# Windowed attention and a mixed feed-forward layer on one Trainium2 core: softmax sums turned by a transposition, and the copy of the rows of maxima one maximum later

## The chip, the cores and the metric

The kernel runs on one core of a Trainium2 chip. The time is that of the device in microseconds (us): the median of several executions, with the lowest and the highest beside it. Engines: PE (TensorE) multiplies and transposes, and loads its weights (PEld) while it does; DVE (VectorE) works elementwise and reduces; ACT (ScalarE) evaluates functions and can issue DMAs; POOL (GpSimd) works elementwise; SP (SyncE) issues DMAs.

## The reference, cut to what matters

```
x : 4 x 2048 x 512
h = layernorm(x);  q, k, v = split(h @ w_qkv)                # 16 heads of 32, 16 windows of 128 tokens
scores[q, key] = (q * 32**-0.5) . k                          # keys: the window before, its own, the one after
attn = softmax(scores, over the keys);  o = attn @ v
x = x + layernorm(o)
x = x + layernorm(ffn(layernorm(x)))                         # weights mixed of 8 experts by a gate, one mix per batch
```

The change lies in the softmax and its normalisation: for each query the maximum of its scores is taken off before the exponential, and the output is divided by the sum of the exponentials.

## The kernel before, in words

The program has three stages. Up to about 570 us it makes q, k and v; each operand is kept as a high and a low part and every product as three. From there to about 1305 us it does attention. The rest is the gate and the feed-forward layer, which the diff doesn't touch.

**The attention loop.** The work is cut into 16 rounds (4 batches by 4 groups of 4 heads), each round into 8 steps of two windows: 128 steps, each with 2 x 4 = 8 units (window, head). The order is written out by hand, engine by engine. The loop `for T in range(STEPS + LAG)` stands once for each engine, and in its pass T several steps are under way:

- **Step T+3: scores and maxima.** PE multiplies queries by keys (`score`, L628) into three PSUM banks used in turn; DVE takes each unit's negated maximum (`reduce`, L493). Score s waits for maximum s-3, whose bank it takes. A unit has 384 keys, or 256 in the first and the last window of a batch.
- **Step T+2: maxima turned.** PE transposes the 128 x 8 maxima into `ps_turn` (`turn_max`, L655) and DVE copies the 8 rows to SBUF (`copy_rows`, L501, then `rows_done`). `send_row` (L196) puts them by DMA under the queries, in partition 96 of `q_st`, the row of window 0 of the step from ACT and that of window 1 from SP. Both wait for `rows_done` first. On ACT it stands behind the fifth exponential (x = 4) of the pass, and x = 5, 6 and 7 stand behind it.
- **Step T: keys by queries, exponentials.** PE multiplies again with the operands exchanged and with the row of maxima as a 97th row, so that the maximum comes off in the product (`keys`, L647), into three other banks; ACT takes exp (`weights`, L421). Product x waits for exponential x-3, also across steps: products 0, 1 and 2 of the next step wait for exponentials 5, 6 and 7 of this one. Product 0 of a step waits for SP's row, product 4 for ACT's row of the step after.
- **Step T-2: values, sums, output.** PE multiplies values by exponentials (`values`, L676) and, from the totals that POOL adds up, makes the sums (`sums`, L684): row 32h+i of `ps_out[:, 2]` has the sums of head h and window i, other rows are zero. ACT copies all to `out_t` (`copy_out`, L428). `turn_out` transposes the two windows (L694) and turns the sums with a product by `pick`, a 128 x 8 selection matrix (L695); it waits for `rows_done` of step T+2, since both use `ps_turn`. DVE inverts the 8 columns of sums (`normalise`, L505) and multiplies (L509); SP stores.

PE's order in a pass: score 0, product 0, score 1, products 1 and 2, score 2, values and sums, `turn_max`, score 3, product 3, score 4, products 4 and 5, scores 5 and 6, product 6, `turn_out`, product 7, score 7. DVE's: maxima 0, 1, 2, the copy of rows, maxima 3 to 7, `normalise`. ACT's: exponentials 0, 1, 2, `copy_out`, exponentials 3 and 4, the DMA of a row, exponentials 5, 6, 7.

Of the kernel before, what the change touches and what calls it, by code (L numbers as in the profile page):

```python
# [5 lines left out]
ALU = mybir.AluOpType  # L6
ACT = mybir.ActivationFunctionType
AX_X = mybir.AxisListType.X
F32 = mybir.dt.float32
F32R = mybir.dt.float32r  # L10

P = 128
D = 512
HEADS = 16
E = D // HEADS
# [7 lines left out]
QH = 4  # L23
# [20 lines left out]
def attention_programs(nc, ident, eps, power, unused, x, w_qkv, qk_dram, v_dram, o_dram):  # L44
# [15 lines left out]
    UNITS = 2 * QH  # L60
    FRONT = AHEAD * UNITS // GROUPS
    PIECES = (0, P, D, 2 * D, 3 * D)
    with ExitStack() as ctx:
        def sb(name, shape, dt, stack=ctx):
            return stack.enter_context(nc.sbuf_tensor("a_" + name, shape, dt))
# [5 lines left out]
            return nc.alloc_semaphore("a_" + name)  # L71

        neg_max = sb("neg_max", [P, 2, 2, QH], F32)
        pick = sb("pick", [P, 2 * QH], F32)
        inv_sum = sb("inv_sum", [P, 2, 2 * QH], F32)
        ones = sb("ones", [P, 2, E], F32)
        max_rows = sb("max_rows", [2 * QH, 2, WIN], F32R)
        q_st = sb("q_st", [P, QH, SEQ], F32R)
# [2 lines left out]
        ps_turn = psum("ps_turn", [P, 4, WIN])  # L81
# [23 lines left out]
        out_t = sb("out_t", [P, 2, 3, WIN], F32)  # L105
        out = sb("out", [P, 2, 2, QH * E], F32)
# [37 lines left out]
        const_done = sem("const_done")  # L144
# [13 lines left out]
        inv_done = sem("inv_done")  # L158
        norm_done = sem("norm_done")
        out_turned = sem("out_turned")  # L160
# [130 lines left out]
        def gpsimd(pool, along):  # L291
            pool.memset(ident[:, :], 0.0).then_inc(front_const, 1)
            pool.memset(eps[:, :], EPS).then_inc(front_const, 1)
            pool.memset(power[:, :], -0.5).then_inc(front_const, 1)
            pool.wait_ge(front_const, 3)
            pool.affine_select(out=ident[:, :], in_=ident[:, :], compare_op=ALU.not_equal, fill=1.0,
                               base=0, pattern=[[-1, P]], channel_multiplier=1).then_inc(front_const, 1)

            for s in range(SLOTS):
                pool.sem_inc(qk_stored[s], 16)  # L300
            for p in range(2):
                pool.sem_inc(v_stored[p], 16 * QUADS)
            pool.memset(ones[:, :, :], 0.0).then_inc(const_done, 1)
            pool.wait_ge(const_done, 1)
            for i in range(2):
                pool.memset(ones[:, i, i:i + 1], 1.0).then_inc(const_done, 1)
                pool.wait_ge(const_done, 2 + i)
            pool.memset(pick[:, :], 0.0).then_inc(const_done, 1)
            pool.wait_ge(const_done, 4)
            pool.affine_select(out=pick[:, :], in_=pick[:, :], compare_op=ALU.not_equal, fill=1.0,  # L310
                               base=0, pattern=[[-1, 2], [-E, QH]], channel_multiplier=1).then_inc(const_done, 1)
            pool.wait_ge(const_done, 5)
            pool.wait_ge(xn_done, 1)
            pool.memset(k_st[STACK:STACK + 1, :, :].bitcast(F32), 1.0).then_inc(const_done, 1)

            def parts(m):
                w = m % W
                lo, hi = span(w)
                return [probs[:, (m - w + kb) % PROBS, :, (w - span(kb)[0]) * WIN:(w - span(kb)[0] + 1) * WIN]
                        for kb in range(lo, hi)]  # L320

            def first_two(g, i):
                m = 2 * g + i
                lo, hi = span(m % W)
                p = parts(m)
                pool.wait_ge(exp_done, QH * (m - m % W + lo + 2))
                if g >= 2:
                    pool.wait_ge(pv_done, g - 1)
                add = pool.tensor_tensor(total[:, g % 2, i], p[0], p[1], ALU.add)  # L329
                add.then_inc(part_summed if len(p) > 2 else summed, 1)  # L330

            def third(g, i):
                m = 2 * g + i
                lo, hi = span(m % W)
                p = parts(m)
                if len(p) > 2:
                    pool.wait_ge(exp_done, QH * (m - m % W + hi))
                    pool.wait_ge(part_summed, threes(m))
                    pool.tensor_tensor(total[:, g % 2, i], total[:, g % 2, i], p[2], ALU.add).then_inc(summed, 1)  # L339

            for g in range(STEPS):
                along(g)
                first_two(g, 0)
                if g % HALF == HALF - 1:
                    third(g, 0)
                    first_two(g, 1)
                else:
                    first_two(g, 1)
                    third(g, 0)
                    third(g, 1)  # L350
# [93 lines left out]
        def vector(dve, along):  # L444
# [57 lines left out]

            def normalise(g):
                dve.wait_ge(out_turned, g + 1)
                dve.reciprocal(inv_sum[:, g % 2, :], ps_turn[:, 3, 0:2 * QH]).then_inc(inv_done, 1)  # L505
                dve.wait_ge(inv_done, g + 1)
                if g >= 2:
                    dve.wait_ge(out_stored[g % 2], 16 * (g // 2))
                dve.tensor_tensor(out[:, g % 2].rearrange("p w (h e) -> p (w h) e", h=QH),  # L509
                                  ps_turn[:, 1:3, :].rearrange("p w (h e) -> p (w h) e", h=QH),  # L510
                                  inv_sum[:, g % 2, :].unsqueeze(2).to_broadcast([P, 2 * QH, E]),
                                  ALU.mult).then_inc(norm_done, 1)

            dve.wait_ge(x_half_loaded, 16)
# [34 lines left out]
                    copy_rows(1)  # L549
            for T in range(STEPS + LAG):  # L550
                if there(T + AHEAD):
                    for s in range(3):
                        reduce(T + AHEAD, s)
                if there(T + AHEAD - 1):
                    copy_rows(T + AHEAD - 1)
                if there(T + AHEAD):
                    for s in range(3, UNITS):
                        reduce(T + AHEAD, s)
                if there(T - LAG):
                    normalise(T - LAG)  # L560
                along(T)

        def tensor(pe, along):
# [124 lines left out]
            def turn_out(g):  # L688
                pe.wait_ge(out_copied, g + 1)
                pe.wait_ge(rows_done, min(g + LAG + AHEAD, STEPS))  # L690
                if g >= 1:
                    pe.wait_ge(norm_done, g)
                for i in range(2):
                    pe.transpose(ps_turn[:, 1 + i, :], out_t[:, g % 2, i, :], ident[:, :])  # L694
                pe.matmul(ps_turn[:, 3, 0:2 * QH], out_t[:, g % 2, 2, :], pick[:, :],  # L695
                          start=True, stop=True, skip_group_check=True).then_inc(out_turned, 1)

            def scores(T, units):
                if there(T + AHEAD):
# [9 lines left out]
            for k in range(KD):  # L709
                for t in range(TILES):  # L710
                    mm = pe.transpose(opening[k][:, t * P:(t + 1) * P], xn[:, t, k * P:(k + 1) * P], ident[:, :])
                mm.then_inc(turned, 1)
            pe.wait_ge(w_lo_done, 1)
            for k in range(KD):
# [3 lines left out]
                mm = pe.matmul(acc[0][:, :], w_lo[:, k, 0:P], xt_hi[:, 0, k, :], start=False, stop=(k == KD - 1))  # L718
# [9 lines left out]
                chunk(i, 0)  # L728
                chunk(i, 1)
            chunk(PAIRS - 1, 0)  # L730
            pe.wait_ge(const_done, 6)
            for g in range(GROUPS):
                group(CHUNKS - 1, 1, g)
                for y in range(FRONT * g, FRONT * (g + 1)):
# [1282 lines left out]
```

## Time and profile before

| | |
|---|---|
| time, median of 3 runs | 2935.83 us (2935.25 to 2944.34) |
| the profiled execution: its own time | 2944.44 us |
| the profiled execution: its span, first to last instruction | 2942.7 us |
| PE busy | 2878.3 us, 98% |
| PE weight loads busy | 2399.2 us, 82% |
| DVE busy | 1994.3 us, 68% |
| ACT busy | 1733.9 us, 59% |
| POOL busy | 856.6 us, 29% |
| chain that ended last, by engine | PE 86%, DMA 6%, DVE 4%, ACT 2% |

How to read it: a busy time is the union of an engine's instructions. A matmul's record starts when it is taken up, which can be before its weights are in, and its end is modelled; so PE can be waiting for a moment inside a busy stretch, and the loads (PEld) show that better. A "q" behind an engine's name (ACTq) is its sequencer, which issues DMAs. "Idle before" is the engine's idle time in front of an instruction and what ended it.

### The profile page before, as it was taken

To read this page: it belongs to the slowest core of one execution; us is meant where nothing else is said; L and a number is where in the kernel's file an instruction comes from. 1 tells how busy PE (TensorE), PEld (TensorE's weight loads), DVE (VectorE), ACT (ScalarE), POOL (GpSimd) and SP (SyncE) were. 2 spreads that over 40 slices of the span, in tenths; PEclk is the share of its full clock that TensorE was granted. 3 is DMA by queue.
4 is the path that set the end of the run, shared out by engine and by line. 5 is a ranking of instruction groups with operands and counts; after the bars stand their busy time and mean duration, and the time that the engine had idled before them with its cause. 6 is when DMAs were issued, how large, how long until landed. Compare 5 with 4: busy or idle time off the path is not lost.

```text
span 2942.7 us, 55697 instructions
## 1 busy us (share of the span) xinstructions
PE 2878.3 (98%) x20380; PEld 2399.2 (82%) x20380; DVE 1994.3 (68%) x3769; ACT 1733.9 (59%) x3385; POOL 856.6 (29%) x715
## 2 busy tenths in 40 slices
PE   8999999999999999989989999999999999999998
PEld 6888888788888888777867888888888888888886
DVE  5333333488888887778868766886769766786664
ACT  3222222367776766666546666766667666686666
POOL 1000000188888887874400000400005000040003
PEclk9999999999999999999999999999999999999999
DMA  6554555688788879959998866986769765895642
GB/s 215 185 171 171 186 188 193 215 193 197 191 199 197 196 193 219 220 167 393 400 389 327 295 208 221 348 324 204 245 212 404 272 204 201 287 390 201 233 136 86
DMA packets 361430, 697.11 MB, mean 237 GB/s; under 512 B 26576, under 2 KB 127056, under 8 KB 361184
## 3 DMA queue, kind: packets, MB, share of 16 engines
q1 hardware_dynamic: 335456, 629.63, 66.8%
q10 hardware_dynamic: 17424, 32.24, 3.1%
q0 software_dynamic: 8304, 31.98, 2.7%
q8 instruction: 151, 2.47, 0.4%
q14 instruction: 95, 0.78, 0.1%
HBM read 525.45 MB, written 167.78 MB: 236 GB/s over the span
## 4 chain that ended last, share of the span: by engine, by line
PE 86%; DMA 6%; DVE 4%; ACT 2%; issue 1%; POOL 1%; ACTq 0%; SPq 0%; DVEq 0%; POOLq 0%
PE a_acc L577 17%; PE e_hid L1397 8%; PE e_hid L1399 8%; PE e_hid L1398 8%; PE e_acc L1414 8%; PE e_acc L1416 8%; PE e_acc L1415 8%; PE a_ps_score L628 6%; PE a_ps_keys L647 6%; PE a_ps_out L676 5%; DMA a_q_st<-a_max_rows 2%; DMA a_gate_att<-o_scratch 2%; PE a_ps_out L684 2%; DVE a_gate_stats L1665 1%; PE a_turn L572 1%
## 5 line engine op out<-in xcount | busy, mean ns | idle before, releaser
L1787 DVE SCALAR_TENSOR_TENSOR e_part<-e_ring,e_g_cols,e_part 128x512 f32<-128x512 f32 x896 | 644.8, 775 | 5.2 <-DMA e_ring<-mix_rows 2.8
L493 DVE TENSOR_REDUCE a_neg_max<-a_ps_score 128x1 f32<-128x384 f32 (+1 forms) x1024 | 491.6, 527 | 63.0 <-PE a_ps_score L628 51.9
L329 POOL TENSOR_TENSOR a_total<-a_probs 128x512 f32<-128x512 f32 x256 | 323.9, 1282 | 592.4 <-ACT a_probs L421 592.2
L421 ACT ACTIVATE a_probs<-a_ps_keys 128x384 f32<-128x384 f32 (+1 forms) x1024 | 429.6, 477 | 53.9 <-PE a_ps_keys L647 24.2
L1811 DVE TENSOR_TENSOR e_u_lo<-e_u,e_u_hi 128x512 fp32r<-128x512 f32 x256 | 180.6, 706 | 372.0 <-ACT e_u_hi L1545 371.9
L1541 ACT ACTIVATE e_u<-e_hid,e_mb 128x512 f32<-128x512 f32 x256 | 176.9, 691 | 427.7 <-PE e_hid L1399 418.2
L1270 POOL TENSOR_SCALAR e_var<-e_moments 128x4 f32<-128x4 f32 x15 | 6.7, 447 | 1269.6 <-DVE e_moments L1823 1269.0
L628 PE MATMUL a_ps_score<-a_k_st,a_q_st 96*128 96x384 f32 (+1 forms) x1024 | 333.9, 361 | 3.5 <-DMA a_q_st<-qk_scratch 2.5
L647 PE MATMUL a_ps_keys<-a_q_st,a_k_st 97*128 97x384 f32 (+1 forms) x1024 | 314.8, 350 | 12.2 <-DMA a_q_st<-a_max_rows 11.1
L339 POOL TENSOR_TENSOR a_total<-a_total,a_probs 128x512 f32<-128x512 f32 x224 | 286.3, 1280 | 67.0 <-ACT a_probs L421 64.3
L473 DVE TENSOR_TENSOR a_qk<-a_acc,a_qk 128x512 fp32r<-128x512 f32 x128 | 88.1, 690 | 308.1 <-ACT a_qk L370 308.1
L1558 ACT ACTIVATE e_sums<-e_acc 128x512 f32<-128x512 f32 x508 | 289.2, 595 | 8.3 <-PE e_acc L1416 5.1
L1569 ACT ACTIVATE e_acc<-e_sums 128x512 f32<-128x512 f32 x448 | 263.7, 614 | 0.0
L370 ACT ACTIVATE a_qk<-a_acc 128x512 fp32r<-128x512 f32 x128 | 76.2, 598 | 259.0 <-PE a_acc L577 255.6
L628 PEld LDWEIGHTS a_ps_score<-a_k_st,a_q_st 96*128 96x128 f32 x1024 | 193.0, 191 | 36.3 <-DVE a_neg_max L493 22.7
L647 PEld LDWEIGHTS a_ps_keys<-a_q_st,a_k_st 97*128 97x128 f32 x1024 | 192.4, 192 | 24.1 <-DMA a_q_st<-a_max_rows 15.4
L577 PE MATMUL a_acc<-a_xt_hi,a_w_hi 128*128 128x512 f32 x508 | 202.5, 399 | 1.1 <-DVE a_qk L473 0.6
L1397 PE MATMUL e_hid<-e_y_hi,e_wb_hi 128*128 128x512 f32 x512 | 200.1, 391 | 2.5 <-DVE e_wb_lo L1806 2.5
L1414 PE MATMUL e_acc<-e_wb_hi,e_u_hi 128*128 128x512 f32 x512 | 199.9, 390 | 1.2 <-ACT e_acc L1569 1.1
L1397 PE MATMUL e_hid<-e_y_hi,e_wa_hi 128*128 128x512 f32 x512 | 200.2, 391 | 0.0
L1414 PE MATMUL e_acc<-e_wa_hi,e_u_hi 128*128 128x512 f32 x512 | 199.4, 389 | 0.7 <-issue 0.6
L1399 PE MATMUL e_hid<-e_y_hi,e_wa_lo 128*128 128x512 f32 x512 | 199.9, 390 | 0.0
(158 smaller groups left out, 6508.5 us busy)
## 6 DMA issues: line engine op xcount, KB each, us to landing
e_ring<-mix_rows SPq DMA_DIRECT2D x558, 512.0 KB, 5.5
qk_scratch<-a_qk SPq DMA_DIRECT2D x128, 512.0 KB, 3.2
a_k_st<-qk_scratch SPq DMA_DIRECT2D x180, 256.0 KB, 4.4
a_q_st<-qk_scratch SPq DMA_DIRECT2D x180, 256.0 KB, 4.4
v_scratch<-a_v SPq DMA_DIRECT2D x64, 256.0 KB, 3.0
a_v_sb<-v_scratch SPq DMA_DIRECT2D x64, 256.0 KB, 4.9
o_scratch<-a_out SPq DMA_DIRECT2D x128, 128.0 KB, 2.9
x_scratch<-a_gate_x POOLq DMA_DIRECT2D x16, 1024.0 KB, 10.0
```

Of the source, the lines that this page charges most:

```text
L329: add = pool.tensor_tensor(total[:, g % 2, i], p[0], p[1], ALU.add)
L339: pool.tensor_tensor(total[:, g % 2, i], total[:, g % 2, i], p[2], ALU.add).then_inc(summed, 1)
L421: act.activation(probs[:, m % PROBS, h, 0:(hi - lo) * WIN], ps_keys[x % TRIO][:, 0:(hi - lo) * WIN], ACT.Exp, scale=SCALE).then_inc(exp_do ...
L493: dve.tensor_reduce(neg_max[:, g % 2, i, h:h + 1], ps_score[y % TRIO][:, 0:(hi - lo) * WIN], AX_X, ALU.max, negate=True).then_inc(reduced, 1)
L577: mm = pe.matmul(out, lhs, rhs, start=(n == 0), stop=(n == len(terms) - 1))
L628: pe.matmul(ps_score[y % TRIO][:, 0:(hi - lo) * WIN], q_st[0:STACK, h, w * WIN:(w + 1) * WIN], k_st[0:STACK, h, lo * WIN:hi * WIN], start= ...
L647: pe.matmul(ps_keys[x % TRIO][:, 0:(hi - lo) * WIN], k_st[0:STACK + 1, h, w * WIN:(w + 1) * WIN], q_st[0:STACK + 1, h, lo * WIN:hi * WIN], ...
L1397: pe.matmul(hid[s % 4][:, :], w_hi(n)[:, 0, cols], y_hi[:, slot, k, :], start=(k == 0), stop=False)
L1399: mm = pe.matmul(hid[s % 4][:, :], w_lo(n)[:, 0, cols], y_hi[:, slot, k, :], start=False, stop=(k == KD - 1))
L1414: pe.matmul(acc[t][:, :], u_hi[:, s % 3, cols], w_hi(n)[:, 1, :], start=False, stop=False, skip_group_check=True)
L1558: act.activation(sums[:, runs[r][1], t, :], acc[t][:, :], ACT.Copy).then_inc(copied, 1)
L1787: dve.scalar_tensor_tensor(out=part[:, n % 2, half, :], in0=ring[:, slot, :], scalar=g_cols[:, b, e:e + 1], in1=so_far, op0=ALU.mult, op1= ...
```

## The change

The third column block of `turn_out` becomes a transposition like the other two; `pick`, its building on POOL and its share of the counts of `const_done` go; the reciprocal reads the sums where the transposition leaves them (column 32h+i) and writes them in order of windows. DVE's copy of the rows moves from behind maximum 2 to behind maximum 3.

```diff
--- before.py
+++ after.py
@@ -71,8 +71,7 @@
             return nc.alloc_semaphore("a_" + name)
 
         neg_max = sb("neg_max", [P, 2, 2, QH], F32)
-        pick = sb("pick", [P, 2 * QH], F32)
-        inv_sum = sb("inv_sum", [P, 2, 2 * QH], F32)
+        inv_sum = sb("inv_sum", [P, 2, 2, QH], F32)
         ones = sb("ones", [P, 2, E], F32)
         max_rows = sb("max_rows", [2 * QH, 2, WIN], F32R)
         q_st = sb("q_st", [P, QH, SEQ], F32R)
@@ -305,11 +304,6 @@
             for i in range(2):
                 pool.memset(ones[:, i, i:i + 1], 1.0).then_inc(const_done, 1)
                 pool.wait_ge(const_done, 2 + i)
-            pool.memset(pick[:, :], 0.0).then_inc(const_done, 1)
-            pool.wait_ge(const_done, 4)
-            pool.affine_select(out=pick[:, :], in_=pick[:, :], compare_op=ALU.not_equal, fill=1.0,
-                               base=0, pattern=[[-1, 2], [-E, QH]], channel_multiplier=1).then_inc(const_done, 1)
-            pool.wait_ge(const_done, 5)
             pool.wait_ge(xn_done, 1)
             pool.memset(k_st[STACK:STACK + 1, :, :].bitcast(F32), 1.0).then_inc(const_done, 1)
 
@@ -502,13 +496,13 @@
 
             def normalise(g):
                 dve.wait_ge(out_turned, g + 1)
-                dve.reciprocal(inv_sum[:, g % 2, :], ps_turn[:, 3, 0:2 * QH]).then_inc(inv_done, 1)
+                dve.reciprocal(inv_sum[:, g % 2], ps_turn[:, 3, :].rearrange("p (h e) -> p e h", e=E)[:, 0:2, :]).then_inc(inv_done, 1)
                 dve.wait_ge(inv_done, g + 1)
                 if g >= 2:
                     dve.wait_ge(out_stored[g % 2], 16 * (g // 2))
                 dve.tensor_tensor(out[:, g % 2].rearrange("p w (h e) -> p (w h) e", h=QH),
                                   ps_turn[:, 1:3, :].rearrange("p w (h e) -> p (w h) e", h=QH),
-                                  inv_sum[:, g % 2, :].unsqueeze(2).to_broadcast([P, 2 * QH, E]),
+                                  inv_sum[:, g % 2].rearrange("p w h -> p (w h)").unsqueeze(2).to_broadcast([P, 2 * QH, E]),
                                   ALU.mult).then_inc(norm_done, 1)
 
             dve.wait_ge(x_half_loaded, 16)
@@ -549,12 +543,12 @@
                     copy_rows(1)
             for T in range(STEPS + LAG):
                 if there(T + AHEAD):
-                    for s in range(3):
+                    for s in range(4):
                         reduce(T + AHEAD, s)
                 if there(T + AHEAD - 1):
                     copy_rows(T + AHEAD - 1)
                 if there(T + AHEAD):
-                    for s in range(3, UNITS):
+                    for s in range(4, UNITS):
                         reduce(T + AHEAD, s)
                 if there(T - LAG):
                     normalise(T - LAG)
@@ -690,10 +684,9 @@
                 pe.wait_ge(rows_done, min(g + LAG + AHEAD, STEPS))
                 if g >= 1:
                     pe.wait_ge(norm_done, g)
-                for i in range(2):
-                    pe.transpose(ps_turn[:, 1 + i, :], out_t[:, g % 2, i, :], ident[:, :])
-                pe.matmul(ps_turn[:, 3, 0:2 * QH], out_t[:, g % 2, 2, :], pick[:, :],
-                          start=True, stop=True, skip_group_check=True).then_inc(out_turned, 1)
+                for i in range(3):
+                    mm = pe.transpose(ps_turn[:, 1 + i, :], out_t[:, g % 2, i, :], ident[:, :])
+                mm.then_inc(out_turned, 1)
 
             def scores(T, units):
                 if there(T + AHEAD):
@@ -728,7 +721,7 @@
                 chunk(i, 0)
                 chunk(i, 1)
             chunk(PAIRS - 1, 0)
-            pe.wait_ge(const_done, 6)
+            pe.wait_ge(const_done, 4)
             for g in range(GROUPS):
                 group(CHUNKS - 1, 1, g)
                 for y in range(FRONT * g, FRONT * (g + 1)):
```

## Rows read from the trace of the kernel before

Times in a timeline are us from the span's start. Pass 62 of the attention loop is the one whose `turn_max` starts at 910.79 us, pass 63 starts so at 916.33, 61 at 905.39 and 60 at 900.04.

**Rows 1.** The page's head line.
```profile
span 2942.7 us, 55697 instructions
```

**Rows 2.** Busy time by engine, 640 to 1150 us (columns named in the first line).
```profile
core 0: us, PE busy (x) PEld busy (x) DVE busy (x) ACT busy (x) POOL busy (x), PEclk, DMA share, GB/s
640.00:1150.00 510.00, 506.85 (x7732) 439.57 (x7731) 419.81 (x1027) 358.03 (x842) 437.21 (x350) 1.00 0.82 197
```

**Rows 3.** Timeline, PE and its weight loads: start, duration (us), work, count, [idle before].
```profile
910.79 0.08 PEld L655 LDWEIGHTS a_ps_turn<-ident,a_neg_max 128*8 128x8 f32 x1 [0.20 <-issue]
...
910.83 0.42 PE L628 MATMUL a_ps_score<-a_k_st,a_q_st 96*128 96x384 f32 x1
...
912.00 0.19 PEld L628 LDWEIGHTS a_ps_score<-a_k_st,a_q_st 96*128 96x128 f32 x1 [0.20 <-DVE a_neg_max L493]
...
912.28 0.34 PE L647 MATMUL a_ps_keys<-a_q_st,a_k_st 97*128 97x384 f32 x1
...
912.46 0.38 PE L694 MATMUL a_ps_turn<-ident,a_out_t 128*128 128x128 f32 x2
...
912.68 0.17 PE L695 MATMUL a_ps_turn<-a_pick,a_out_t 128*128 128x8 f32 x1
...
913.08 0.34 PE L628 MATMUL a_ps_score<-a_k_st,a_q_st 96*128 96x384 f32 x1
...
913.82 0.19 PEld L647 LDWEIGHTS a_ps_keys<-a_q_st,a_k_st 97*128 97x128 f32 x1
...
914.07 0.19 PEld L628 LDWEIGHTS a_ps_score<-a_k_st,a_q_st 96*128 96x128 f32 x1
...
914.44 0.11 PEld L676 LDWEIGHTS a_ps_out<-a_probs,a_v_sb 128*32 128x32 f32 x2 [0.19 <-issue]
...
916.33 0.08 PEld L655 LDWEIGHTS a_ps_turn<-ident,a_neg_max 128*8 128x8 f32 x1 [0.20 <-issue]
```

**Rows 4.** Timeline, DVE, the same step.
```profile
911.21 0.28 DVE L501 CAST a_max_rows<-a_ps_turn 8x128 fp32r<-8x128 f32 x1 [0.75 <-PE a_ps_turn L655]
...
911.41 0.53 DVE L493 TENSOR_REDUCE a_neg_max<-a_ps_score 128x1 f32<-128x384 f32 x1
...
911.88 0.54 DVE L493 TENSOR_REDUCE a_neg_max<-a_ps_score 128x1 f32<-128x384 f32 x1
...
913.46 0.56 DVE L493 TENSOR_REDUCE a_neg_max<-a_ps_score 128x1 f32<-128x384 f32 x1
```

**Rows 5.** Timeline, ACT, the same step.
```profile
911.82 0.58 ACTq L196 DMA_DIRECT2D a_q_st<-a_max_rows  x1
...
912.45 0.49 ACT L421 ACTIVATE a_probs<-a_ps_keys 128x384 f32<-128x384 f32 x1
...
912.83 0.48 ACT L421 ACTIVATE a_probs<-a_ps_keys 128x384 f32<-128x384 f32 x1
...
913.28 0.49 ACT L421 ACTIVATE a_probs<-a_ps_keys 128x384 f32<-128x384 f32 x1
```

**Rows 6.** Timeline, DVE and SP, the step before it.
```profile
905.80 0.28 DVE L501 CAST a_max_rows<-a_ps_turn 8x128 fp32r<-8x128 f32 x1 [1.22 <-PE a_ps_turn L655]
...
906.01 0.40 DVE L493 TENSOR_REDUCE a_neg_max<-a_ps_score 128x1 f32<-128x256 f32 x1
...
906.11 0.58 SPq L196 DMA_DIRECT2D a_q_st<-a_max_rows  x1
```

**Rows 7.** Timeline, other kinds of step, DVE, ACT and PE weight loads.
```profile
900.45 0.28 DVE L501 CAST a_max_rows<-a_ps_turn 8x128 fp32r<-8x128 f32 x1 [0.75 <-PE a_ps_turn L655]
...
903.51 0.13 PEld L676 LDWEIGHTS a_ps_out<-a_probs,a_v_sb 128*32 128x32 f32 x4 [0.20 <-issue]
...
908.91 0.12 PEld L676 LDWEIGHTS a_ps_out<-a_probs,a_v_sb 128*32 128x32 f32 x3 [0.18 <-ACT a_probs L421]
...
917.93 0.66 ACT L421 ACTIVATE a_probs<-a_ps_keys 128x256 f32<-128x256 f32 x2 [0.17 <-issue]
...
919.85 0.12 PEld L676 LDWEIGHTS a_ps_out<-a_probs,a_v_sb 128*32 128x32 f32 x3 [0.18 <-ACT a_probs L421]
```

**Rows 8.** Waits, 600 to 1270 us: total, times, longest (us).
```profile
PEld a_ps_keys L647 <- DMA a_q_st<-a_max_rows: 13.9, 13, 3.1
```

## The prediction

> **What bounds the kernel now.** I read the busy times of a stretch of the attention loop first, then the timeline of one pass engine by engine, then the waits. The stretch shows PE busy 506.85 of 510 us at a granted clock of 1.00, DVE 419.81, ACT 358.03, POOL 437.21 [rows 2]. PE looks like the only bound, and a change that shortens PE's work should pay in full. But PE's record covers stalls: what is to be seen is in the loads. In pass 62 (5.54 us, from 910.79 to 916.33) the load of score 6 starts at 912.00 after 0.20 idle, released by DVE [rows 3]: maximum 3 ran from 911.41 to 911.95 [rows 4]. The load of the next product 2 starts at 913.82 [rows 3], 0.05 after exponential 7 ended at 913.77 (913.28 + 0.49) [rows 5]. The load of the next score 2 starts at 914.07 [rows 3], 0.05 after maximum 7 ended at 914.02 [rows 4]. So PE is handed from one engine to another three times a pass, with almost nothing to spare: a gain on PE alone goes only as far as the next of these.
>
> **Turn-out on PE.** Two transpositions take 0.38 us and one 0.27 (its length when alone, mostly latency), so they follow each other at 0.11. The two passes of the pick product begin at 912.68; product 7 behind them really begins 0.175 before score 7, whose matmul starts at 913.08 (0.175 is the pace of a 384-key matmul: product 6 at 912.28, first transposition at 912.46). That is 912.91, so the pick product costs 0.23 [rows 3]. A third transposition costs 0.11 at the pace of the two, with its own 128 x 128 load like theirs. Saved on PE: 0.12 a pass. The cost is bounded from both sides by 0.11 (that pace) and 0.23 (no gain, if it took two passes as the product does); I take 0.11, the row of the same operation.
>
> **Reciprocal, multiplication, constants.** The reciprocal still makes 8 values per partition, now read 32 apart; between nothing and a few hundredths, on DVE where 0.75 us are idle before each copy [rows 4]. POOL's two instructions for `pick` run before the first layernorm is done, and PE asks for the constants only at the last chunk: nothing.
>
> **Copy behind maximum 3, on DVE.** Now the copy starts at 911.21 and maximum 3 at 911.41, 0.20 behind; maxima follow at 0.46 (911.41, 911.88) and take 0.54 [rows 4]. After the change maximum 3 starts as soon as score 3 is there: its matmul ends at 910.83 + 0.42 = 911.25 [rows 3], and DVE needs 0.04 more (score 7 ends at 913.42, maximum 7 starts at 913.46) [rows 3, 4]. So maximum 3 runs 911.29 to 911.82, 0.13 earlier; score 6 no longer stalls for it (a gain of about 0.13 on PE). The copy starts 0.46 behind, 911.75, and ends at 912.03, where it ended at 911.49: 0.54 later. Maximum 4 starts 0.20 behind it, 911.95 (before 911.88), maximum 7 at 913.35 if score 7 is there, and PE, 0.25 ahead by then, has it there. It ends at 913.90 (before 914.02): by DVE, score 2 could go 0.11 earlier.
>
> **Who waits for the copy.** Three: SP's DMA, PE's turn-out, ACT's DMA. *SP*: its row goes out 0.54 later and is wanted almost a pass and a half later; `store` behind it in SP's queue waits for `normalise` anyway. *PE*: turn-out may start from about 912.09; score 6 and product 6 bring PE there at about 912.15. Hidden, with 0.06 to spare. *ACT*: its DMA starts at 911.82, as soon as exponential 4 has been handed over, takes 0.58, and exponential 5 starts at 912.45, 0.05 behind its end; exponentials 5 and 6 are 0.38 apart [rows 5]. So ACT already loses 0.2 a pass to the issue, and everything behind the DMA waits with it. By a row of the step before, a DMA that waited for the copy starts 0.03 after it (copy 905.80 + 0.28, SP's DMA 906.11) [rows 6]. After the change ACT's DMA can't start before 912.03 + 0.03 = 912.06, 0.24 later than now. It ends at 912.64, exponential 5 starts at 912.69, 6 at 913.07, 7 at 913.46 (product 7 is long there), ending at 913.95. The load of the next product 2 then starts at 914.00 instead of 913.82. That is the new stall.
>
> No row of before has ACT waiting in front of its DMA, so what such a wait holds up is not shown. The Trainium skill (DMA: Bandwidth & Descriptors, Anatomy of one DMA) says the wait of a DMA is done on the issuing sequencer, which agrees with my reading. The same section puts the dispatch at about 50 ns; the row has 0.58 us, and the row decides. With 50 ns exponential 5 would not be delayed at all, and the sum would be that of the first rival.
>
> **The sum for an ordinary pass.** A stalled load lets its matmul begin 0.11 after it starts (load of score 6 at 912.00, product 6 at 912.28 less 0.175) [rows 3]. Now: score 2 at 914.07 + 0.11 = 914.18. After: product 2 at 914.11, score 2 0.175 later, 914.285. Values, sums and the next `turn_max` follow in fixed distance (914.44, 916.33). Change: **+0.10 us**, against the 0.25 that PE gained and the 0.11 that DVE allowed. Passes 0, 1, 2, 3 and 6 of a round are of this kind: +0.52.
>
> **The other passes of a round.** In pass 4 maxima of 256 keys let PE run on: values start 3.47 after `turn_max` (903.51, and 900.45 - 0.41 = 900.04) [rows 7], in pass 62 3.65. ACT's chain is as long as in pass 62, and puts them at 3.65 + 0.10 less 0.05 for the shorter score 2: +0.22. In pass 5 maximum 3 takes 0.40 [rows 6] and its score is 0.06 shorter, so the copy ends earlier (1.04 after `turn_max`, not 1.24) and ACT's delay is 0.1: values at 3.55 against 3.52 (905.39, 908.91) [rows 7]: +0.03. In pass 7 the exponentials behind the DMA have 256 keys and follow at 0.28 [rows 7]; ACT would be done in time, DVE ends maximum 7 as late as now; values at 3.52 (919.85) [rows 7] stay: 0. A round: 0.52 + 0.22 + 0.03 = 0.77 us, 16 rounds: **+12.3 us**.
>
> **Rows landing late.** Product 4 waited 13 times for a row to land, 13.9 us in all [rows 8]. ACT's row leaves 0.24 later while the pass grows by 0.10, so each such wait deepens by 0.14, 1.8 us; nothing at the low end, 6 us at the high end if rows that just make it now fall behind (twice as many waits, each 0.24). I take +1.8.
>
> Sum: +14 us. The profiled execution took 2944.44 us for a span of 2942.7 [rows 1], and goes to 2958.5; it is 8.6 above the median of the runs shown, 2935.83, which goes to **2950**. About 0.3% (9 us) is what a measurement of this kernel can tell from no change.
>
> **Rivals.**
> *ACT's DMA holds nobody up* (faster). If ACT had its slack elsewhere, or exponentials 5 to 7 could go on, DVE would be next: score 2 0.11 earlier in five passes, about 0.1 in passes 4 and 5, none in 7: 0.75 a round, -12 us, 2924. For it: PE's and DVE's rows both allow it. Against: exponential 5 starts 0.05 behind the DMA's end in every pass. It decides once the delay on ACT is under the slack of product 2 and score 2, about 0.13; it needs the copy to end before 911.92, and even with no latency at all (911.25 + 0.46 + 0.28 = 911.99) it doesn't. Chance 0.13.
> *The two cancel* (no change). The ACT chain is shorter than I have it by up to 0.1, as when exponentials close up to 0.35 behind one another; 2931 to 2943. Chance 0.19.
> *The copy is held till maximum 3 is finished* (slower still). Rows show the next DVE instruction 0.07 before the end of the last [rows 4], but always of maxima. Then ACT is 0.07 later in seven passes of eight, +8 us, and PE's turn-out loses its 0.06 of cover as well: 2958. Chance 0.15. The Trainium skill (VectorE: DVE Perf Modes, The DRAIN you can't avoid) has the next instruction wait for the pipe to empty, which would be this case; the overlap of the maxima speaks against it.
> *The third transposition is no cheaper than the pick product*: no effect on the sum, since PE waits for ACT by then; it is inside the forecast.
>
> **The numbers.** The forecast has 0.53, the case still slower 0.15, no change 0.19, faster 0.13. Slower by over 0.3%: 0.53 + 0.15 less what falls below 2944.6, and some of the cancelling case above it: 0.68. Range 2932 to 2962: from most of the cancelling case to late rows on top of the held copy; it leaves the faster rival out.
>
> **What would show it.** In the changed kernel's ordinary pass: maximum 3 starts 0.49 after `turn_max` and the copy at 0.95; ACT's DMA at 1.26 instead of 1.03; exponential 5 at 1.89 instead of 1.66; no idle before the load of score 6; a new wait of product loads on exponentials; turn-out in three steps of 0.11; pass length 5.63 instead of 5.54, and 5.58 instead of 5.36 in pass 4. It would be wrong if exponential 7 ended less than 3.04 after `turn_max`, or if the DMA of ACT took less than 0.58.

## The result, and the profile after

| | before | after |
|---|---|---|
| time, median (lowest to highest) | 2944.03 us (2935.25 to 2951.69, 8 runs) | 2953.94 us (2946.92 to 2958.25, 8 runs) |
| ratio to before | | **1.0029**, 95% interval 1.0015 to 1.0043 |
| profiled execution: own time, span | 2944.44, 2942.7 us | 2950.66, 2948.8 us |

The change makes the kernel slower, by 8.5 us (0.0029 x 2944), between 4.4 and 12.7. The median of before over eight runs is 8 us above that of the three runs known ahead of the prediction; the ratio counts.

The page after, against [rows 1]: the head line, the busy times, and the two groups in which something new stands.

```profile
span 2948.8 us, 55438 instructions
...
PE 2882.6 (98%) x20252; PEld 2375.6 (81%) x20252; DVE 1986.2 (67%) x3769; ACT 1719.0 (58%) x3385; POOL 854.6 (29%) x713
...
L487 DVE TENSOR_REDUCE a_neg_max<-a_ps_score 128x1 f32<-128x384 f32 (+1 forms) x1024 | 495.0, 528 | 168.4 <-PE a_ps_score L622 166.7
...
L641 PEld LDWEIGHTS a_ps_keys<-a_q_st,a_k_st 97*128 97x128 f32 x1024 | 190.1, 190 | 55.2 <-ACT a_probs L415 23.4
```

The maxima (L487) now have 166.7 us of idle time before them that scores ended; in front of the copy there was such idle time before [rows 4]. The loads of products (L641) wait for exponentials (L415), a wait that was hardly there before. The busy times in the stretch of [rows 2]:

```profile
core 0: us, PE busy (x) PEld busy (x) DVE busy (x) ACT busy (x) POOL busy (x), PEclk, DMA share, GB/s
640.00:1150.00 510.00, 507.39 (x7588) 419.15 (x7584) 406.53 (x1014) 340.47 (x829) 433.64 (x347) 1.00 0.81 193
```

PE looks just as busy as before (507.39 against 506.85 us): this view doesn't show the loss. ACT and DVE get fewer instructions done in the same 510 us (829 against 842, and 1014 against 1027). Pass 62, PE and its loads, against [rows 3]:

```profile
917.93 0.08 PEld L649 LDWEIGHTS a_ps_turn<-ident,a_neg_max 128*8 128x8 f32 x1 [0.20 <-issue]
...
919.03 0.19 PEld L622 LDWEIGHTS a_ps_score<-a_k_st,a_q_st 96*128 96x128 f32 x1
...
919.48 0.49 PE L688 MATMUL a_ps_turn<-ident,a_out_t 128*128 128x128 f32 x3
...
920.20 0.19 PEld L622 LDWEIGHTS a_ps_score<-a_k_st,a_q_st 96*128 96x128 f32 x1 [0.20 <-issue]
...
921.12 0.19 PEld L641 LDWEIGHTS a_ps_keys<-a_q_st,a_k_st 97*128 97x128 f32 x1 [0.20 <-ACT a_probs L415]
...
923.55 0.08 PEld L649 LDWEIGHTS a_ps_turn<-ident,a_neg_max 128*8 128x8 f32 x1 [0.20 <-issue]
```

The pass takes 5.62 us from `turn_max` to `turn_max` (before 5.54). The load of score 6 comes 1.10 after `turn_max` (before 1.21), and three transpositions take 0.49, that is 0.11 more than two. Then the gain goes: the load of the next score 0 comes 0.20 after the engine fell idle ("issue": the view names no releaser; maximum 5, which it needs, had just ended at 920.09), and the load of product 2, at 3.19, waits 0.20 for an exponential; before it came at 3.03. DVE, against [rows 4]:

```profile
918.42 0.56 DVE L487 TENSOR_REDUCE a_neg_max<-a_ps_score 128x1 f32<-128x384 f32 x1 [1.06 <-PE a_ps_score L622]
...
918.89 0.27 DVE L495 CAST a_max_rows<-a_ps_turn 8x128 fp32r<-8x128 f32 x1
...
920.48 0.54 DVE L487 TENSOR_REDUCE a_neg_max<-a_ps_score 128x1 f32<-128x384 f32 x1
```

Maximum 3 starts at 0.49, the copy at 0.96, its end is at 1.23; maximum 7 starts at 2.55. ACT, against [rows 5]:

```profile
919.19 0.58 ACTq L195 DMA_DIRECT2D a_q_st<-a_max_rows  x1
...
919.82 0.49 ACT L415 ACTIVATE a_probs<-a_ps_keys 128x384 f32<-128x384 f32 x1 [0.35 <-PE a_ps_keys L641]
...
920.58 0.50 ACT L415 ACTIVATE a_probs<-a_ps_keys 128x384 f32<-128x384 f32 x1
```

The DMA starts at 1.26 (before 1.03), 0.03 behind the copy's end. ACT then sits idle 0.35 us while its sequencer issues, exponential 5 starts at 1.89 and exponential 7 at 2.65, ending at 3.15. The view names "PE a_ps_keys" for the idle time of exponential 5, but product 5 had ended long before; it is the DMA in front of it. The waits from 600 to 1270 us, the second row against [rows 8]:

```profile
PEld a_ps_keys L641 <- ACT a_probs L415: 20.2, 103, 0.2
...
PEld a_ps_keys L641 <- DMA a_q_st<-a_max_rows: 17.3, 17, 1.9
...
PEld a_ps_score L622 <- DVE a_neg_max L487: 2.8, 15, 0.2
```

The same view of before:

```profile
PEld a_ps_score L628 <- DVE a_neg_max L493: 19.9, 91, 0.4
...
PEld a_ps_keys L647 <- ACT a_probs L421: 0.2, 1, 0.2
```

Products now wait 103 times for an exponential, 20.2 us, where it was once; scores wait for maxima 15 times, 2.8 us, where it was 91 times and 19.9 us.

### The profile page after: what moved, and what is told of

It reads as the page before. It is cut to its first block, busy times and chain, and to the rows that moved or that the text cites. A ratio compares the mean times of both kernels' runs of the same rounds, so it can differ in the third digit from the quotient of the medians.

```text
span 2948.8 us, 55438 instructions
## 1 busy us (share of the span) xinstructions
PE 2882.6 (98%) x20252; PEld 2375.6 (81%) x20252; DVE 1986.2 (67%) x3769; ACT 1719.0 (58%) x3385; POOL 854.6 (29%) x713
## 4 chain that ended last, share of the span: by engine, by line
PE 84%; DMA 6%; DVE 5%; issue 2%; ACT 2%; POOL 1%; ACTq 0%; SPq 0%; DVEq 0%; POOLq 0%
PE a_acc L571 17%; PE e_acc L1407 7%; PE e_hid L1390 7%; PE e_hid L1392 7%; PE e_hid L1391 7%; PE e_acc L1408 7%; PE e_acc L1409 7%; PE a_ps_keys L641 6%; PE a_ps_score L622 6%; PE a_ps_out L670 5%; DMA a_q_st<-a_max_rows 3%; DMA a_gate_att<-o_scratch 2%; PE a_ps_out L678 2%; PE a_ps_turn L688 1%; DVE e_part L1780 1%
## 5 line engine op out<-in xcount | busy, mean ns | idle before, releaser
L487 DVE TENSOR_REDUCE a_neg_max<-a_ps_score 128x1 f32<-128x384 f32 (+1 forms) x1024 | 495.0, 528 | 168.4 <-PE a_ps_score L622 166.7
L415 ACT ACTIVATE a_probs<-a_ps_keys 128x384 f32<-128x384 f32 (+1 forms) x1024 | 413.6, 479 | 65.7 <-PE a_ps_keys L641 58.1
L641 PE MATMUL a_ps_keys<-a_q_st,a_k_st 97*128 97x384 f32 (+1 forms) x1024 | 336.3, 364 | 15.8 <-DMA a_q_st<-a_max_rows 12.2
L641 PEld LDWEIGHTS a_ps_keys<-a_q_st,a_k_st 97*128 97x128 f32 x1024 | 190.1, 190 | 55.2 <-ACT a_probs L415 23.4
L1391 PE MATMUL e_hid<-e_y_lo,e_wa_hi 128*128 128x512 f32 x512 | 199.8, 390 | 0.0
```

The costliest lines, as they stand in the source:

```text
L415: act.activation(probs[:, m % PROBS, h, 0:(hi - lo) * WIN], ps_keys[x % TRIO][:, 0:(hi - lo) * WIN], ACT.Exp, scale=SCALE).then_inc(exp_do ...
L487: dve.tensor_reduce(neg_max[:, g % 2, i, h:h + 1], ps_score[y % TRIO][:, 0:(hi - lo) * WIN], AX_X, ALU.max, negate=True).then_inc(reduced, 1)
L641: pe.matmul(ps_keys[x % TRIO][:, 0:(hi - lo) * WIN], k_st[0:STACK + 1, h, w * WIN:(w + 1) * WIN], q_st[0:STACK + 1, h, lo * WIN:hi * WIN], ...
L1391: pe.matmul(hid[s % 4][:, :], w_hi(n)[:, 0, cols], y_lo[:, slot, k, :], start=False, stop=False)
```

## The experiments

Each ratio is against the kernel before, run on the same chip. "A round" is the sum over the 8 kinds of pass of the median distance between `turn_max` starts in that kernel's profile; times 16 it gives the price of the passes alone. (In e3 the median of pass 2, 5.67 us, is raised by passes that wait; up to `turn_max` 104 it is 5.49.) The columns on the right split one profiled execution at `turn_max` 10, 104 and 127, with the granted clock of the last stretch. `turn_max` n turns the maxima of step n and lies in pass n-2; it is at pass 102, behind `turn_max` 104, that SP begins to load for the gate beside the attention loop.

| kernel | turn | copy behind | ACT's row | a round, us | x16, against before | measured ratio (interval) | 10 to 104, us | 104 to 127, us | clock, 104 to 127 |
|---|---|---|---|---|---|---|---|---|---|
| before | pick | 2 | behind x=4 | 43.40 | | | 512.2 | 146.5 | 0.93 |
| after | transposed | 3 | x=4 | 44.16 | +12.1 | 1.0029 (1.0015, 1.0043) | 520.4 | 138.8 | 1.00 |
| e1 | transposed | 2 | x=4 | 42.63 | -12.3 | 0.9970 (0.9959, 0.9980) | 504.3 | 141.1 | 0.98 |
| e8 (as e1) | transposed | 2 | x=4 | 42.62 | -12.5 | 0.9978 (0.9968, 0.9989) | 506.1 | 149.0 | 0.92 |
| e2 | pick | 3 | x=4 | 44.18 | +12.4 | 1.0027 (1.0017, 1.0038) | 519.5 | 139.0 | 0.99 |
| e3 | transposed | 3 | from SP | 42.91 | -7.8 | 0.9985 (0.9976, 0.9993) | 507.2 | 144.5 | 0.94 |
| e4 | transposed | 3 | x=5 | 42.77 | -10.1 | 0.9982 (0.9973, 0.9990) | 504.6 | 144.3 | 0.95 |
| e5 | transposed | 4 | x=4 | 47.63 | +67.6 | 1.0201 (1.0184, 1.0218) | 560.6 | 146.9 | 0.97 |
| e6 | pick | 3 | from SP | 42.97 | -7.0 | 1.0007 (0.9995, 1.0018) | 509.9 | 138.7 | 0.99 |
| e7 | transposed | 2 | x=3 | 43.17 | -3.8 | 0.9992 (0.9983, 1.0001) | 508.3 | 143.7 | 0.94 |
| e9 | transposed | 2 | x=5 | 42.52 | -14.2 | 0.9973 (0.9964, 0.9981) | 501.9 | 151.1 | 0.92 |
| e10 | transposed | 2 | from SP | 42.54 | -13.8 | 0.9984 (0.9974, 0.9993) | 504.7 | 144.7 | 0.94 |

### The two parts alone (e1, e8, e2)

e1 and e8, the same kernel measured on two chips, are the changed kernel with the copy back at its place:

```diff
-                    for s in range(4):
+                    for s in range(3):
                         reduce(T + AHEAD, s)
                 if there(T + AHEAD - 1):
                     copy_rows(T + AHEAD - 1)
                 if there(T + AHEAD):
-                    for s in range(4, UNITS):
+                    for s in range(3, UNITS):
                         reduce(T + AHEAD, s)
```

> The sums turned by the third transposition, the copy of the rows left behind maximum 2. Theory (ACT's row DMA, which waits for the copy, is what costs in the full change): the DMA starts at 1.03 after turn_max as before, so the 0.115 us saved on PE in the turn-out goes through: score 7 and with it maximum 7 come 0.115 earlier, ACT's chain still has room (exponential 7 ends at 2.92, it may end at 2.95). Ordinary pass 5.42 us instead of 5.53, kernel 10 to 14 us faster than before, ratio 0.995 to 0.997. Rival (a gain on PE is worth nothing in this loop, because DVE and ACT hand work to it): pass 5.53, ratio 1.000. Second rival (the third transposition is what makes the full change slower): ratio over 1.002.

> The third transposition alone once more, as the measure for the two runs beside it: ratio 0.996 to 0.998, ordinary pass 5.42 us. Both theories say the same of it.

Pass 62 of e1, `turn_max`, the load of the next score 2 and the next `turn_max`:

```profile
904.74 0.08 PEld L649 LDWEIGHTS a_ps_turn<-ident,a_neg_max 128*8 128x8 f32 x1 [0.20 <-issue]
...
907.91 0.19 PEld L622 LDWEIGHTS a_ps_score<-a_k_st,a_q_st 96*128 96x128 f32 x1
...
910.17 0.08 PEld L649 LDWEIGHTS a_ps_turn<-ident,a_neg_max 128*8 128x8 f32 x1 [0.20 <-issue]
```

5.43 us, and score 2 at 3.17 (before 3.27), 0.05 behind maximum 7. The transposition alone saves 0.11 us an ordinary pass, all that it saves on PE, and the ratios are 0.9970 and 0.9978. The rivals fall: PE's gain counts, and the transposition isn't what costs.

e2 is the kernel before with the same edit the other way round.

> The copy behind maximum 3, the sums turned by the pick product as before. Theory: ACT's chain sets the pass, which does not see the turn-out: DMA of the row at 1.26, exponential 5 at 1.89, pass 5.63 us, the same as in the full change; kernel 12 us slower than before (ratio 1.004), within 2 us of the full change. Rival (the two parts add, each with its own price on PE): the full change less the gain of the transposition, pass 5.75, 20 to 26 us slower, ratio 1.007 to 1.009.

A round is 44.18 us against 44.16 of the full change, the ratio 1.0027 against 1.0029. With the copy behind maximum 3, and ACT's DMA where it is, the transposition is worth nothing: the parts don't add, ACT sets the pass and the turn-out lies beside it. (1.004 was expected; the passes alone would give it.)

### ACT's wait taken away, two ways (e3, e4)

e3:

```diff
                 if there(T + AHEAD - 1):
-                    send_row(sp, T + AHEAD - 1, 1)
+                    for i in range(2):
+                        send_row(sp, T + AHEAD - 1, i)
...
-                    if x == 4 and there(T + AHEAD - 1):
-                        send_row(act, T + AHEAD - 1, 0)
```

> The full change, with both rows of a step sent by SP and none by ACT. Theory: ACT no longer waits nor issues, exponential 5 starts at 1.44, and product 2 no longer waits for exponential 7. Next is DVE: maximum 6 ends at 2.62 and sets score 1, three matmuls later score 2; ordinary pass 5.47 us, kernel 6 us faster than before (ratio 0.998) and 18 us faster than the full change. Rival (the loss comes from the copy being late for PE's turn-out or from the rows landing late): pass 5.63 or waits of products on DMAs of more than 30 us in all, ratio 1.003 or more, since copy and rows are as late as in the full change or later.

Pass 62 of e3: `turn_max`, exponentials 4 and 5, the load of score 1, the next `turn_max`:

```profile
907.88 0.08 PEld L648 LDWEIGHTS a_ps_turn<-ident,a_neg_max 128*8 128x8 f32 x1 [0.20 <-issue]
...
908.94 0.87 ACT L416 ACTIVATE a_probs<-a_ps_keys 128x384 f32<-128x384 f32 x2
...
910.56 0.19 PEld L621 LDWEIGHTS a_ps_score<-a_k_st,a_q_st 96*128 96x128 f32 x1
...
913.34 0.08 PEld L648 LDWEIGHTS a_ps_turn<-ident,a_neg_max 128*8 128x8 f32 x1 [0.20 <-issue]
```

Exponential 5 follows 4 at once. The load of score 1 comes at 2.68, released by maximum 6 as the theory had it, and the pass takes 5.46. The copy is as late as in the full change and the row that ACT sent leaves no earlier, and the loss is gone.

e4 only moves the DMA behind the next exponential:

```diff
-                    if x == 4 and there(T + AHEAD - 1):
+                    if x == 5 and there(T + AHEAD - 1):
```

> The full change, with ACT's DMA of the row one exponential later, behind x = 5. The issue still costs ACT its 0.58 us, but the wait for the copy (till 1.23) is over by then. Theory: exponential 5 at 1.44, DMA at 1.41 to 1.99, exponential 6 at 2.04, 7 at 2.43, its end at 2.92 sets nothing; ordinary pass 5.47 us like with the rows sent by SP, 6 us faster than before from the passes, given back in part by rows that leave 0.38 later than before (0 to 6 us): ratio 0.998 to 1.000. Rival (it is the cost of issuing on ACT, not the wait in front of it): as the full change, ratio 1.003, pass 5.63.

```profile
905.24 0.08 PEld L649 LDWEIGHTS a_ps_turn<-ident,a_neg_max 128*8 128x8 f32 x1 [0.20 <-issue]
...
906.51 0.58 ACTq L195 DMA_DIRECT2D a_q_st<-a_max_rows  x1
...
906.67 0.50 ACT L415 ACTIVATE a_probs<-a_ps_keys 128x384 f32<-128x384 f32 x1
...
910.71 0.08 PEld L649 LDWEIGHTS a_ps_turn<-ident,a_neg_max 128*8 128x8 f32 x1 [0.20 <-issue]
```

ACT's DMA still starts at 1.27 and takes 0.58, but exponential 5 starts at 1.43, and the pass takes 5.47. What costs is that the wait for the copy, and behind it the 0.58 us of the issue, stand in front of exponential 5; the same issue one place later costs nothing that the pass shows. The late copy by itself costs little: with ACT's DMA at x=4 it makes a round 1.53 us longer (44.16 against 42.63), at x=5 only 0.25 (42.77 against 42.52, e9 below).

### The copy later still (e5)

```diff
-                    for s in range(4):
+                    for s in range(5):
...
-                    for s in range(4, UNITS):
+                    for s in range(5, UNITS):
```

> The full change with the copy of the rows one maximum later still, behind maximum 4. Theory (ACT's DMA waits for the copy): the copy ends at 1.70 after turn_max instead of 1.23, the DMA runs from 1.73 to 2.31, exponential 5 starts at 2.36, 7 ends at 3.61, the load of product 2 starts at 3.66 instead of 3.20: ordinary pass 6.10 us (5.635 in the full change, 5.53 before), a round longer by 3.6 us than in the full change, 58 us in all, so 70 us slower than before from the passes alone, ratio 1.020 to 1.024, the lower end since passes that wait for a landing row anyway have less to lose. Rival (PE's turn-out, which waits for the same copy, sets the pass): it would start 0.32 us later, ordinary pass 5.95, ratio 1.016 or less. Second rival (what costs is one instruction more in front of DVE's copy, not when it ends): 5.74, ratio 1.008.

Pass 62: `turn_max`, the copy, ACT's DMA, the load of the next product 2, the next `turn_max`:

```profile
944.90 0.08 PEld L649 LDWEIGHTS a_ps_turn<-ident,a_neg_max 128*8 128x8 f32 x1 [0.20 <-issue]
...
946.33 0.27 DVE L495 CAST a_max_rows<-a_ps_turn 8x128 fp32r<-8x128 f32 x1
...
946.63 0.58 ACTq L195 DMA_DIRECT2D a_q_st<-a_max_rows  x1
...
948.57 0.19 PEld L641 LDWEIGHTS a_ps_keys<-a_q_st,a_k_st 97*128 97x128 f32 x1 [0.20 <-ACT a_probs L415]
...
951.00 0.08 PEld L649 LDWEIGHTS a_ps_turn<-ident,a_neg_max 128*8 128x8 f32 x1 [0.20 <-issue]
```

The copy starts at 1.43, the DMA at 1.73, product 2 waits for exponential 7 till 3.67, the pass takes 6.10 us. Every time that the theory gave for this pass is there. PE's turn-out does wait for the copy here (its first load starts at 1.77, in after at 1.38), but it would set 5.95; both rivals fall. A round is 3.47 us longer than in the full change (3.6 expected).

### Is the transposition worth something without ACT's wait? (e6)

e6 is e2 with the rows sent by SP, as in e3.

> The copy behind maximum 3 and the sums turned by the pick product, both rows sent by SP. Theory: without ACT's wait DVE sets the pass through maximum 6 and score 1, which lie behind PE's turn-out with time to spare, so the transposition is worth nothing here: pass 5.47 us and ratio 0.998 to 0.999, as with the third transposition. Rival (PE's own time sets the pass once ACT is out of the way): 0.115 us longer, 5.58, ratio 1.002 to 1.003.

Two `turn_max` of an undisturbed pass of the same kind:

```profile
864.82 0.08 PEld L654 LDWEIGHTS a_ps_turn<-ident,a_neg_max 128*8 128x8 f32 x1 [0.20 <-issue]
...
870.29 0.08 PEld L654 LDWEIGHTS a_ps_turn<-ident,a_neg_max 128*8 128x8 f32 x1 [0.20 <-issue]
```

5.47 us, as forecast: in an ordinary pass the transposition is worth nothing here. But the ratio is 1.0007 where 0.998 to 0.999 was expected, and e3 has 0.9985. Passes 4 and 5 are 0.12 and 0.07 us longer than in e3, which explains 3 us of the 6 (16 x 0.19). What makes the rest was not separated.

### The rows' landing (e7, e9, e10)

e7 is e1 with `x == 3` for ACT's DMA.

> The third transposition, the copy behind maximum 2, and ACT's DMA of the row one exponential earlier, behind x = 3, where the copy has just ended: DMA at 0.71 instead of 1.03, exponential 4 at 1.33, 5 at 1.71, 7 ends at 2.97. Theory of the row that lands late (product 4 waits for ACT's row, some 17 us in all when passes are short): rows leave 0.3 us earlier, which takes 5 to 7 us off these waits, against 0.03 us a pass on ACT's chain, 3 us: ratio to before 0.995 to 0.997, at or below that of the transposition alone (0.997), waits of products on rows under 12 us. Rival (these waits are set by the DMA queues' load and not by when the row leaves): waits stay at 17 us or more and the ratio is 0.998.

```profile
908.95 0.08 PEld L649 LDWEIGHTS a_ps_turn<-ident,a_neg_max 128*8 128x8 f32 x1 [0.20 <-issue]
...
909.67 0.58 ACTq L195 DMA_DIRECT2D a_q_st<-a_max_rows  x1
...
910.68 0.48 ACT L415 ACTIVATE a_probs<-a_ps_keys 128x384 f32<-128x384 f32 x1
...
914.41 0.08 PEld L649 LDWEIGHTS a_ps_turn<-ident,a_neg_max 128*8 128x8 f32 x1 [0.20 <-issue]
```

```profile
PEld a_ps_keys L641 <- DMA a_q_st<-a_max_rows: 11.2, 10, 2.7
```

The waits of products on rows fall to 11.2 us as expected, but exponential 5 starts at 1.73 and the pass takes 5.46, not 5.45, and passes 4 and 5 of a round got 0.12 and 0.15 longer, which the expectation had left out: a round costs 0.54 us more than in e1, 8.5 us in all instead of 3. The ratio, 0.9992, where 0.995 to 0.997 was expected (0.998 by the rival), agrees with the price of the passes, 0.9987.

e9 is e1 with `x == 5`; e10 is e1 with the rows from SP.

> The third transposition, the copy behind maximum 2, and ACT's DMA of the row behind x = 5. On ACT the same work stands in front of exponential 7 (it starts at 2.42 in either order), so the ordinary pass stays at 5.42 us; only the row leaves 0.37 us later. Theory of the late rows (what a kernel gains or loses beside its passes is in passes that wait for a row): waits of products on rows rise by 5 to 7 us over the run beside it, ratio 0.002 above it. Rival (the row has time enough, these waits come and go with the chip): ratio as in the run beside it, within 0.001.

The waits of products on rows, first in e9, then in e8 beside it:

```profile
PEld a_ps_keys L641 <- DMA a_q_st<-a_max_rows: 14.6, 18, 2.8
```

```profile
PEld a_ps_keys L641 <- DMA a_q_st<-a_max_rows: 20.3, 16, 2.9
```

The row leaves at 1.20 after `turn_max` instead of 1.03: 0.17 later, not 0.37, since ACT hands exponential 5 over sooner there. So the test was weaker than planned. The waits are shorter in this profile, not longer, and 0.9973 is within 0.001 of 0.9978: no sign that a later departure costs, but half the dose. With e7 on the other side, whether the time of departure sets these waits stays open.

> The third transposition, the copy behind maximum 2, both rows sent by SP. ACT has nothing to issue: exponential 7 no longer sets product 2, and what is left is DVE (maximum 7 ends at 3.11, score 2 at 3.17): ordinary pass 5.42 us as with the transposition alone, passes 4 and 5 of a round shorter by 0.1 or so, 3 us in all. SP sends the row that ACT sent at 0.71 in even passes and about 0.9 in odd ones, behind its loads, so rather earlier than ACT. Theory: ratio 0.994 to 0.996, 3 to 6 us faster than the run beside it. Rival (ACT's issue was hidden, only its wait for the copy cost anything): ratio as in the run beside it, within 0.001.

A round is 0.08 us shorter than in e8 (1.3 us in all, 3 expected), and 0.9984 is not below 0.9978. ACT's issue without the wait was hidden, as the rival said. What three kernels with both rows from SP give back beside their passes, 3.4 us (e3) to 9.1 (e6 and e10), isn't explained. In these three product 4 waits for its row most often, 23 times in e3, 27 in e6 and 24 in e10, against 9 to 20 in the others; no run tests whether that is the reason.

### Where the passes' price went

In each of the eleven comparisons the measured ratio lies on the side of less effect than the price of the passes, by 1 to 9 us (e6 even changes its sign). The split at pass 102 shows where to look. First before, then after, from `turn_max` 10 to 104 and from 104 to 127:

```profile
core 0: us, PE busy (x) PEld busy (x) DVE busy (x) ACT busy (x) POOL busy (x), PEclk, DMA share, GB/s
617.33:1129.54 512.21, 510.48 (x7802) 442.97 (x7799) 422.68 (x1034) 361.28 (x846) 440.71 (x353) 1.00 0.81 195
1129.54:1276.05 146.51, 135.17 (x1908) 115.45 (x1905) 112.46 (x271) 93.92 (x215) 121.39 (x101) 0.93 0.90 216
```

```profile
619.55:1139.94 520.39, 517.78 (x7708) 427.32 (x7705) 415.13 (x1034) 348.18 (x846) 441.11 (x353) 1.00 0.81 193
1139.94:1278.71 138.77, 127.25 (x1885) 104.10 (x1881) 110.07 (x271) 91.66 (x215) 120.65 (x100) 1.00 0.93 226
```

In the first 94 passes the change costs 520.4 - 512.2 = 8.2 us, close to 94/8 x 0.76 = 8.9. The last 23 take 146.5 before and 138.8 after. That is mostly the clock: the granted clock of TensorE was 0.93 in the last stretch of before and 1.00 in that of after. In before it is at 0.50, the lower of its two levels, for some 20 us, beside the three longest waits of PE for a DMA (2.83, 3.09 and 1.97 us). The second of these, and four of the microseconds behind it:

```profile
1183.54 0.29 PEld L647 LDWEIGHTS a_ps_keys<-a_q_st,a_k_st 97*128 97x128 f32 x1 [3.09 <-DMA a_q_st<-a_max_rows]
```

```profile
1186.00:1190.00 4.00, 4.00 (x33) 3.48 (x37) 2.93 (x6) 1.89 (x5) 2.51 (x2) 0.50 0.82 164
```

This pass is 6.9 us longer than the median of its kind, for a wait of 3.1. In after no wait is longer than 1.9 us and the clock stays at 1.00. The column of clocks in the table puts the other kernels in the same order: the last 23 passes take 138.7 to 141.1 us at 0.98 to 1.00, 143.7 to 146.5 at 0.93 to 0.95, 149.0 and 151.1 at 0.92 (e5, whose passes are 0.5 us longer, 146.9 at 0.97). Times the clock, as an estimate of what they would have taken without its loss, they come to about 136.3 before and 138.8 after: 2.5 apart, where 23/8 x 0.76 = 2.2 is the price of the passes. For e5 it is 142.5, 6 us above before where its passes ask for 12, and for e1 138.3, above before where its passes ask for less. So a difference between two profiles in this stretch says little of the change, and the passes' price is paid in it only in part. The clock doesn't explain why the medians fall short: the mean clock of a kernel's executions differs from that of before beside it by at most 0.0007 (0.9934 against 0.9927 for e1, 0.9929 against 0.9936 for e8), which is 2 us, in either direction.

There the DMA engines are busier (0.90 and 0.93 against 0.81) with the loads for the gate beside the rest, and products wait for rows. What such a wait does, in one pass of after: the copy, the load of product 4, ACT's DMA.

```profile
1170.59 0.27 DVE L495 CAST a_max_rows<-a_ps_turn 8x128 fp32r<-8x128 f32 x1
...
1171.88 0.19 PEld L641 LDWEIGHTS a_ps_keys<-a_q_st,a_k_st 97*128 97x128 f32 x1 [1.77 <-DMA a_q_st<-a_max_rows]
...
1172.37 0.58 ACTq L195 DMA_DIRECT2D a_q_st<-a_max_rows  x1
```

The copy ends at 1170.86, but product 4 waits for its row till 1171.88, exponential 4 for product 4, and ACT's DMA goes out at 1172.37, 1.5 us after the copy. In such a pass it doesn't matter when the copy is made. The lengths agree: six passes of before with such a wait are each longer than the median of its kind by about 0.19 us less than the wait (1.46 waited, 1.27 longer, behind `turn_max` 106), and ten of after by about 0.30 less (1.36 and 1.06). So with the same wait the pass is as long in both, and the 0.10 of the change isn't paid. That is under 2 us in all 17 waits of after, and no run shows how much of the rest it makes.

## Why the prediction was right or wrong

- **Direction, mechanism, size.** Slower was forecast with 0.68, by ACT's DMA waiting for the copy. The pass: maximum 3 forecast at 0.49 and found at 0.49, copy 0.95 and 0.96, DMA 1.26 and 1.26, exponential 5 1.89 and 1.89, product 2's load 3.20 and 3.19, pass 5.63 and 5.62. Between them e2, e3, e4 and e5 tell this mechanism from PE's turn-out, from late rows and from the issue by itself. The rival in which ACT's DMA holds nobody up fell with exponential 5 at 1.89. It was also priced too high: in e3 and e4, where ACT holds nobody up, a round is 0.49 and 0.63 us shorter than before, not 0.75, since maximum 6 then holds score 1, a wait that the prediction left out.
- **Turn-out.** 0.12 saved by the transposition: three take 0.49, against 0.38 for two and 0.23 for the pick product, 0.61; e1 shows it in the time.
- **Copy held?** The rival of a copy held 0.07 till maximum 3 is finished fell: maximum 3 runs 918.42 to 918.98, the copy starts at 918.89. The overlap is as between maxima, so this copy was not made to wait for the pipe to empty. The section of the Trainium skill that the prediction names for that rule (VectorE: DVE Perf Modes, The DRAIN you can't avoid) adds that a next instruction that is not held starts earlier; the prediction left this out, and the trace agrees with it: the copy starts 0.08 us before the end of the maximum.
- **The other passes.** Forecast +0.22, +0.03 and 0 for 4, 5 and 7; medians +0.22, +0.04 and -0.03. A round: 0.77 forecast, 0.76 measured.
- **Rows landing late: the term that was off.** "I take +1.8" assumed that a pass that waits for a row pays the longer pass and a wait 0.14 deeper. The waits did grow, from 13.9 us in 13 times to 17.3 in 17, but not deeper (1.07 and 1.02 us each), and over the kernels run they are 8.0 to 22.0, so one profile can't confirm the size. The longer pass isn't paid there: ACT's DMA stands behind exponential 4 in such a pass, not behind the copy. The whole came to 8.5 (4.4 to 12.7): that leaves out the 14 of the sum, and not the 12.1 of the passes alone. That the true size is below 12.1 rests on all eleven comparisons falling on that side; why stays open in part.
- **The 50 ns.** In the Trainium skill (DMA: Bandwidth & Descriptors, Anatomy of one DMA) this dispatch stands in a list for DMAs on GpSimd's path; ACT's took 0.58 us here, and exponential 5 was delayed by it.
- **The absolute number.** 2950 against 2953.94 is nearer than the working deserves: the base was 8 us too low and the size 14 for 8.5, and the two errors partly cancel, which is luck. Against the base of eight runs the forecast would have been 2958. Slower by over 0.3% had a chance of 0.68; the ratio came out on that border.

## What to carry to other kernels

When an instruction is moved later on one engine, list every queue that waits for its semaphore, and in each the instructions behind the waiting one: here VectorE and TensorE both gained, and ScalarE, busy only 70% of the stretch, lost more because a 2 KB DMA in its order waited for the copy. The remedy is one line, the DMA behind the next exponential (e4, 0.9982), or to take the transposition alone: at 0.9970 and 0.9978 it beats both kernels. A price worked out from undisturbed passes holds only for them; a pass that already waits for a transfer may not pay it. And before two profiles are compared stretch by stretch, compare the granted clock of the stretch: here the slower kernel took 7.7 us less in one stretch, at a clock of 1.00 against 0.93.

## What was not expected of the hardware

- A DMA that waits in ScalarE's order delays the next exponential until the wait is over and its 0.58 us of issue have run: ScalarE was idle 0.35 us, although nothing that this exponential reads was missing.
- Beside the gate's loads 23 passes took 138.7 to 151.1 us, in the order of the granted clock (1.00 to 0.92) more than of what a pass cost elsewhere: around waits of 2 to 3 us TensorE's clock was granted at half, and such a pass lost up to 6.9 us instead of 3.1.
- A row of 2 KB was waited for 8 to 22 us in all in the kernels run, most often where SP sent both rows (23 to 27 times), and otherwise in no clear order by when it was sent.
